# A DLRM tower on one core: zeros written on GpSimd behind each of the later gathers

## What is computed

```python
e = jnp.stack([tbl_0[ids[:, 0]], ..., tbl_25[ids[:, 25]]], axis=1)      # 512 x 26 x 128
sd = jnp.einsum('bfd,bd->bf', e, dense)
ss = jnp.einsum('bfd,bgd->bfg', e, e)                                    # pairs f < g are kept
z = concatenate([dense, sd, ss[:, iu, ju]], axis=1)
h = concatenate([z, dense], axis=1)                                      # 607 columns
h = maximum(h @ W_top1 + b_top1, 0.0)                                    # 512 columns
h = maximum(h @ W_top2 + b_top2, 0.0)                                    # 256 columns
y = h @ W_top3                                                           # 1 column
```

## Time and profile before

| | us |
|---|---|
| median of 3 runs | 103.39 (103.14 to 104.42) |
| the profiled execution | 103.16 |
| its span, first to last instruction | 101.4 |
| TensorE busy | 88.2 (87% of the span) |
| GpSimd busy, with the gaps between its gathers not counted | 64.8 |
| mean granted TensorE clock | 0.966 of full speed |

### The profile page before, as it was taken

One profiled execution on the slowest core, in us unless ns is written; L12 is line 12 of the kernel. 1 busy time (PEld: TensorE's weight loads), 2 busy tenths in 40 slices (PEclk: granted clock), 3 DMA queues, 4 the chain that ended last, 5 costly groups with the idle time before them and its releaser, 6 DMA issues.

```text
span 101.4 us, 3379 instructions
## 1 busy us (share of the span) xinstructions
PE 88.2 (87%) x1434; PEld 74.7 (74%) x1434; DVE 75.5 (74%) x182; ACT 61.8 (61%) x131; POOL 64.8 (64%) x70
## 2 busy tenths in 40 slices
PE   3977679999999999999957296899999798997990
PEld 4956358888888888878747286798888787996870
DVE  0369599999999999998006797797777769888411
ACT  1632529649649829709726597977777839766110
POOL 2678777777777777787777777777777777100000
PEclk9999999999999999999996559999999999999999
DMA  1869996963963999611222122222222122100000
GB/s 27 227 227 405 384 379 161 375 210 84 357 177 66 345 389 349 185 52 26 55 58 61 52 58 52 58 58 52 61 61 58 49 70 57 32 6 3 0 0 1
DMA packets 6609, 13.50 MB, mean 133 GB/s; under 512 B 1985, under 2 KB 3266, under 8 KB 6594
## 3 DMA queue, kind: packets, MB, share of 16 engines
q1 hardware_dynamic: 4256, 9.08, 25.8%
q0 software_dynamic: 2048, 4.20, 15.1%
q10 hardware_dynamic: 290, 0.01, 0.2%
HBM read 13.28 MB, written 0.00 MB: 131 GB/s over the span
## 4 chain that ended last, share of the span: by engine, by line
PE 69%; ACT 8%; DMA 8%; issue 6%; DVE 3%; SPq 2%; DVEq 0%
PE hidden L361 18%; PE gram L361 14%; PE gram L390 14%; DMA raw<-in_tables_one 8%; PE hidden L417 7%; PE stage L345 7%; ACT Z L518 5%; PE second L436 5%; DVE Z L595 2%; PE hidden L406 2%; ACT ET L496 2%; PE stage L417 1%; ACT part L485 1%; SPq L276 1%; DVE part L585 1%
## 5 line engine op out<-in xcount | busy, mean ns | idle before, releaser
L314 POOL DMA_INDIRECT rows<-in_tables_gather,idx x64 | 64.1, 1002 | 20.9 <-issue 18.9
L595 DVE COPY Z<-gram 32x112 f32<-32x112 f32 (+3 forms) x72 | 23.1, 321 | 9.9 <-PE gram L390 8.9
L578 DVE TENSOR_SCALAR onehot<-ids,rowid 128x1024 fp32r<-128x1024 int16 (+1 forms) x48 | 29.3, 662 | 1.6 <-DMA ids<-in_ids_one 1.6
L518 ACT COPY Z<-gram 32x112 f32<-32x112 f32 (+1 forms) x72 | 23.3, 324 | 10.9 <-PE gram L390 10.1
L361 PE MATMUL hidden<-onehot,part 128*128 128x512 f32 x80 | 20.5, 401 | 1.3 <-DVE onehot L578 0.8
L361 PE MATMUL gram<-onehot,part 128*128 128x512 f32 x80 | 20.0, 398 | 1.1 <-DVE onehot L578 1.1
L390 PE MATMUL gram<-ET 128*32 128x27 f32 x1024 | 14.6, 204 | 6.2 <-issue 4.7
L390 PEld LDWEIGHTS gram<-ET 128*32 128x32 f32 x1024 | 12.3, 120 | 8.5 <-issue 6.4
L361 PEld LDWEIGHTS hidden<-onehot,part 128*128 128x128 f32 x80 | 14.4, 188 | 5.2 <-DVE onehot L578 1.6
L361 PEld LDWEIGHTS gram<-onehot,part 128*128 128x128 f32 x80 | 14.7, 189 | 4.5 <-DVE onehot L578 1.5
L585 DVE TENSOR_TENSOR part<-raw,part 128x512 fp32r<-128x512 f32 (+2 forms) x20 | 13.3, 682 | 2.0 <-ACT part L485 1.0
(11 more groups left out here) (43 smaller groups left out, 48.8 us busy)
## 6 DMA issues: line engine op xcount, KB each, us to landing
raw<-in_tables_one SPq DMA_DIRECT2D x9, 512.0 KB, 5.1
ids<-in_ids_one SPq DMA_DIRECT2D x4, 256.0 KB, 7.0
rows<-in_tables_gather,idx POOLq DMA_INDIRECT x64, 3.9
W1s<-in_W_pairs SPq DMA_DIRECT2D x1, 768.0 KB, 7.7
W1d<-in_W_dense SPq DMA_DIRECT2D x1, 512.0 KB, 5.0
W2s<-in_W_top SPq DMA_DIRECT2D x1, 512.0 KB
raw<-in_tables_one SPq DMA_DIRECT2D x1, 384.0 KB, 3.8
ids<-in_ids_one SPq DMA_DIRECT2D x2, 128.0 KB, 4.1
```

The lines of the kernel that those rows point to most:

```text
L314: pool.indirect_dma_start(out=rows[:, m % ROWS_RING, :], out_offset=None, in_=x["tables_gather"], in_offset=bass.IndirectOffsetOnAxis(ap=i ...
L518: last = act.copy(dst, src)
L578: dve.tensor_scalar(onehot[:, m % RING, 0:w], ids16[:, B * SIDE[g][0]:B * SIDE[g][0] + w], rowid[:, k:k + 1], None, ALU.is_equal).then_inc ...
L595: last = dve.tensor_copy(dst, src)
```

## The change

From block 8 on, which is from gather 32 of 64, GpSimd issues a memset of a new tile `spare` (128 partitions x 256 columns of fp32) behind every gather. Nothing reads `spare`. Since each memset writes the same bytes, each but the first waits on the semaphore `spaced` until the one before it has ended. No other engine's instructions change, and no transfer is added.

```diff
+SPACED = 8
+SPACE = 256
...
+        spare = sb("spare", [P, SPACE])
...
+        spaced = sem("spaced")
...
         def _(pool):
+            spaces = [0]
+
             def gather(n, k):
...
                     in_offset=bass.IndirectOffsetOnAxis(ap=idx[:, m:m + 1], axis=0),
                 ).then_inc(gathered[n], 16)
+                if n >= SPACED:
+
+                    if spaces[0]:
+                        pool.wait_ge(spaced, spaces[0])
+                    pool.memset(spare[:, :], 0.0).then_inc(spaced, 1)
+                    spaces[0] += 1
```

## The result

The changed kernel takes **108.98 us** (median of 4 runs, 108.68 to 109.41) against 103.36 us before. The ratio is 1.0525, with a 95% interval of 1.0445 to 1.0605: slower, by 5.4 to 5.6 us. The profiled execution took 108.68 us, 5.52 more than before, and its span is 106.8 us, 5.4 more.

What follows compares the result with a forecast made beforehand. TensorE was taken to bound the kernel, with GpSimd's gathers about half a microsecond behind. Profiled 103.16 us plus 8.7 for delayed gathers plus 1.0 for the clock gave 112.9, forecast as 113.0 us, range 108 to 121.

Steps and rivals of the forecast that it cites:

- the case that had a chance of 0.65: Prediction's main case: each memset adds 0.2 to 0.45 us to the gather step, giving 108.8 to 117.6 us.
- two chains half a microsecond apart: TensorE sets the time, with GpSimd's gathers right behind from b13 on; b15 lands 0.59 us before its use.
- moved start of gather 63, less 0.6: The end moves by the last gather's delay less b15's slack: 31 d - 0.6, forecast 8.7 us.
- The length of the memset: On GpSimd, a memset of 256 columns was forecast to take 0.31 us.
- d: What one memset adds to GpSimd's step from gather to gather; taken as 0.30 us.
- it begins only when the engine's work is done, and work put ahead of it moves it: Claim that the 0.30 us gap ahead of each gather follows the memset undiminished; the reason for d = 0.30.
- the rival with a partial memset: Memset overlaps the gather on GpSimd and only its end shows: d 0.09 to 0.2, 107.3 us at 0.15; chance 0.10.
- The rival of the hidden memset: Memset runs inside the 0.30 us gap ahead of each gather: d near 0, time stays 103.2 us; chance 0.08.
- The clock: TensorE's wait for b13 should bring its low clock, costing between nothing and 2.8 us; taken as 1.0.
- The waits: TensorE waits 1.3 us for b11, 1.2 for b12, 4.0 for b13, 0.6 for b14, 1.6 for b15.
- The ring: Gathers wait for transposes of the block three earlier, landed two blocks of gathers before; forecast no further wait.
- The floor: Time is at least b15's landing plus 12.8 us plus 1.76 outside the span: 102.57 us with no added delay.

Runs made afterwards that it cites:

- cols512: Changed kernel with memsets of 512 columns instead of 256: 116.57 us, ratio 1.1257 to the kernel before.
- first_half: Changed kernel with memsets only behind the gathers of b8 to b11, 16 instead of 32: 105.72 us, ratio 1.0220 to the kernel before.
- second_half_b: Changed kernel with memsets only behind the gathers of b12 to b15, 16 instead of 32: 105.77 us, ratio 1.0218 to the kernel before.
- no_wait112: Changed kernel with memsets of 112 columns on 32 partitions, each on its own place, without waits: 105.21 us, ratio 1.0155 to the kernel before.
- from0: Changed kernel with memsets of 256 columns behind all 64 gathers instead of the last 32: 119.72 us, ratio 1.1579 to the kernel before.
- cols1: Changed kernel with memsets of 1 column instead of 256: 103.84 us against 103.24 for the kernel before, ratio 1.0009.
- upper_half: Changed kernel with memsets writing partitions 64 to 127 only, still 256 columns: 108.84 us, ratio 1.0519 to the kernel before.
- again: The changed kernel unaltered, run in another session: 108.79 us, ratio 1.0509 to the kernel before.
- bunched: Changed kernel with its 32 memsets four in a row behind each block's last gather: 128.06 us against 130.67 for the kernel before, ratio 0.9797.
- cols128: Changed kernel with memsets of 128 columns instead of 256, on a chip where the kernel before takes 131.29 us: ratio 0.9994.

## Why the prediction was right, and where it was off

The forecast was 113.0 us with a range of 108 to 121, and 108.98 was measured. The direction and the bound were right. The size was not: 9.7 us were added for the profiled execution and 5.5 came, and the result lies only 1 us inside the low end of the range. That it lies inside owes something to luck, since the cost of one memset came out below the values of the case that had a chance of 0.65.

- **The bound.** Right: two chains half a microsecond apart. The sum "moved start of gather 63, less 0.6" holds in every run with a kernel before of 103 us in which gathers were delayed. It gives 5.5, 11.9, 2.7, 2.4, 2.1 and 15.8 us for the changed kernel, cols512, first_half, second_half_b, no_wait112 and from0; the transposes of b15 moved by 5.6, 12.1, 2.8, 2.5, 2.2 and 15.9.
- **The length of the memset.** Forecast 0.31 us from the rows at the start of the trace, measured 0.33.
- **d, the term that was mis-sized.** The step that failed is "it begins only when the engine's work is done, and work put ahead of it moves it". d was 0.197 and not 0.30. That is below the 0.24 us which the prediction gave as the least of the engine's time that stays, and it falls just under its own case (0.2 to 0.45) into the numbers of the rival with a partial memset (0.09 to 0.2). The rows had shown the gap behind gathers only, and a gap that a gather does not cover can still be covered in part by a memset. Of the 0.30 us gap, 0.13 to 0.14 cover a memset and 0.16 to 0.17 stay behind it. cols1 shows it at its plainest, where the whole memset vanished. The rival of the hidden memset was thus half right, and the rival of the partial one had its sign and size but not its place: upper_half shows no overlap with the gather itself.
- **The clock.** Forecast 1.0 between 0 and 2.8. It fell as forecast, behind the wait for b13, and cost nothing, because TensorE waited again for b15. In cols512 1.3 us are lost when it is low behind b15.
- **The waits.** In the profiled execution the wait for b13 was 2.3 us against a forecast of 4.0, and that for b15 1.25 against 1.6; b11, b12 and b14 had none, against 1.3, 1.2 and 0.6. The run "again" spread them otherwise, with 2.86 us at b12, so how they fall on the blocks is more than this forecast could give. With d = 0.197 the sum of the prediction gives b13 4.5 - 0.45 = 4.1 us late in all. TensorE used up a part of it by itself: its clock was low until about 66 us, not 60, and b10 was transposed at 68.4 instead of 66.4.
- **The costs put at nothing.** The ring gave no wait, and the look back over a gather cost nothing (cols1, and no_wait112 agrees). The price named for an uncovered wait, 0.24 us, was too high: 0.04 in bunched.
- **The floor.** No execution of any kernel here took less than the 102.57 us of the floor; the fastest, of the kernel before, took 102.76. No run was built to break the floor, so it is not tested hard.

With d = 0.197 and nothing for the clock, the prediction's sum gives 31 x 0.197 - 0.59 = 5.5 us; 5.52 was measured. So the structure of the sum holds, and d and the clock were the terms of the wrong size.

## What to carry to other kernels

An engine that is absent from the chain that ended last can still be half a microsecond from it. Set the landing of each of its transfers against their use, and take the smallest slack of the last ones: a delay put anywhere ahead is carried on to them, unless the engine has to wait for something in between, as it did for the ring where the kernel before takes 131 us. The gap between two instructions is not all one thing. Whether it covers new work at all is found with an instruction of almost no length, and how much of it does with two longer ones.

## What was not expected of the hardware

- The gap of 0.30 us ahead of a gather on GpSimd takes up to about 0.14 us of a memset at no cost, once for each gap. A memset of 1 column (0.12 us) behind each gather is free.
- A memset of 256 columns takes 0.33 us on GpSimd whether it writes 64 or 128 partitions.
- Beside DVE's one-hot operations a memset costs 0.34 us a step instead of 0.20, and DVE's one-hot operations of 1024 columns take 877 ns on the mean instead of 752.
- In two sessions, on two chips, the same kernel before took 131 us instead of 103. The traces of those sessions show 17 to 23 us of standing still ahead of TensorE's small matmuls, while single operations take what they take elsewhere (in cols128 a DVE copy 320 ns against 321, a gather 1005 against 1002).
